# A decoder layer's feed-forward on one core: up for all tokens, then down, each with seven products in place of eight

## What is computed

```python
def _L0_ffn_ref(x, w1, s1, w2, s2, w3, s3):
    W1 = dequant_q40(w1, s1, hidden, dim)      # hidden = 2752, dim = 1024
    W3 = dequant_q40(w3, s3, hidden, dim)      # 4-bit words times a scale for 64 values
    W2 = dequant_q40(w2, s2, dim, hidden)
    a = jnp.einsum('bsd,hd->bsh', x, W1)
    b = jnp.einsum('bsd,hd->bsh', x, W3)
    h = jax.nn.silu(a) * b
    return jnp.einsum('bsh,dh->bsd', h, W2)
...
x = x + _L0_ffn_ref(_layernorm(x, axis=-1), ...)
```

## Time and profile before

| | |
|---|---|
| median of 3 runs | 3304.04 us (3301.68 to 3304.31) |
| profiled execution, its time from first to last instruction (span) | 3302.6 us |
| profiled span against the median | 1.4 us less |
| PE busy | 3132.5 us, 95% |
| DVE, ACT, POOL busy | 54%, 32%, 15% |
| mean granted clock of PE | 0.976 of full speed |
| stage of the feed-forward | 1806.6 to 3302.6 us |

### The profile page before, as it was taken

One profiled execution on the slowest core, in us unless ns is written; L12 is line 12 of the kernel. 1 busy time (PEld: TensorE's weight loads), 2 busy tenths in 40 slices (PEclk: granted clock), 3 DMA queues, 4 the chain that ended last, 5 costly groups with the idle time before them and its releaser, 6 DMA issues. The chain is left out here.

```text
span 3302.6 us, 41842 instructions
## 1 busy us (share of the span) xinstructions
PE 3132.5 (95%) x15136; PEld 2396.3 (73%) x15136; DVE 1772.9 (54%) x2927; ACT 1045.8 (32%) x2356; POOL 506.7 (15%) x525
## 2 busy tenths in 40 slices
PE   7999998799999999999996799999999899999999
PEld 6888886566666666666663688888887788888887
DVE  5311112466666666666663655555555655555555
ACT  2100000566666566666651211111111211111111
POOL 2100000233333333333332100000000100000000
PEclk9999999899999999999997899999999999999999
DMA  4222223111111111111110422222122521222222
GB/s 143 93 71 74 73 73 109 48 39 38 38 51 48 40 38 39 50 38 51 38 33 25 134 82 54 72 65 80 54 81 73 153 66 54 81 81 54 61 75 78
DMA packets 83350, 218.73 MB, mean 66 GB/s; under 512 B 11984, under 2 KB 18256, under 8 KB 81232
## 3 DMA queue, kind: packets, MB, share of 16 engines
q1 hardware_dynamic: 83280, 217.78, 21.7%
HBM read 175.79 MB, written 41.94 MB: 66 GB/s over the span
## 5 line engine op out<-in xcount | busy, mean ns | idle before, releaser
L1042 ACT ACTIVATE w_hi<-words 128x1024 fp32r<-128x1024 f32 x134 | 142.5, 1064 | 697.5 <-DVE words L1087 697.5
L312 PE MATMUL ff_ps<-h_xT_hi,w_hi 128*128 128x512 f32 x1376 | 344.0, 392 | 13.2 <-DVE h_xT_lo L96 13.2
L1127 DVE TENSOR_TENSOR acc<-ff_po,acc 128x512 f32<-128x512 f32 x352 | 243.0, 692 | 210.0 <-PE ff_po L1214 209.3
L312 PE MATMUL ff_ps<-h_xT_lo,w_hi 128*128 128x512 f32 x1376 | 341.8, 391 | 0.0
L312 PE MATMUL ff_ps<-h_xT_hi,w_lo 128*128 128x512 f32 x1376 | 339.8, 389 | 0.0
L312 PEld LDWEIGHTS ff_ps<-h_xT_hi,w_hi 128*128 128x128 f32 x1376 | 259.8, 189 | 68.4 <-issue 8.8
L312 PEld LDWEIGHTS ff_ps<-h_xT_lo,w_hi 128*128 128x128 f32 x1376 | 260.0, 189 | 54.4
L312 PEld LDWEIGHTS ff_ps<-h_xT_hi,w_lo 128*128 128x128 f32 x1376 | 258.3, 188 | 53.6
L282 DVE TENSOR_SCALAR qkv_out<-qkv_acc 128x512 f32<-128x512 f32 x96 | 66.4, 692 | 396.5 <-PE qkv_acc L312 396.5
L1115 DVE TENSOR_TENSOR gate<-gate,ff_ps 128x512 f32<-128x512 f32 (+1 forms) x88 | 60.3, 686 | 345.4 <-PE ff_ps L312 344.6
L656 ACT ACTIVATE scores<-scores,neg_max 128x128 f32<-128x128 f32 x512 | 199.1, 390 | 122.6 <-DVE neg_max L487 122.6
(11 more groups left out here) (156 smaller groups left out, 5196.5 us busy)
## 6 DMA issues: line engine op xcount, KB each, us to landing
words<-in_w SPq DMA_DIRECT2D x90, 512.0 KB, 3.5
qkv<-qkv_out SPq DMA_DIRECT2D x96, 256.0 KB, 2.0
words<-in_w SPq DMA_DIRECT2D x176, 128.0 KB, 4.0
sc<-in_s SPq DMA_DIRECT2D x88, 256.0 KB, 4.3
qk_in<-qkv SPq DMA_DIRECT2D x16, 1024.0 KB, 5.0
w_stage<-in_w_attn SPq DMA_DIRECT2D x56, 256.0 KB, 2.9
qkv_rows<-in_x SPq DMA_DIRECT2D x16, 512.0 KB, 3.8
ctx_in<-in_context SPq DMA_DIRECT2D x16, 512.0 KB, 3.8
```

What stands on the lines that cost most here:

```text
L312: last = nc.tensor.matmul(out, left, right, start=n == 0, stop=n == len(pairs) - 1)
L1042: nc.scalar.activation(dst, src, ACT.Copy).then_inc(s["split_hi"], 1)
L1127: nc.vector.tensor_tensor(cols, po[:, o % 4, :], cols, ALU.add).then_inc(s["added"], 1)
```

## The change

One level of Strassen's algorithm, in Winograd's form with chained sums, is applied to both products. The stage becomes two passes.

**Up.** A hidden tile's weights W1 and W3 form the columns of a 2 x 2 block matrix whose rows are the two halves of the features; the tokens' block matrix has the two halves of the features and the two halves of the 1024 tokens. Seven products of 4 feature slices x 3 passes give the four PSUM sums. The operands of the products are the blocks and sums of them: three sums of the weights before and one behind `w_low` 4, on POOL (`w_sums`, `w_last_sum`), and four sums of the tokens, once in each half (`x_sums`). ACT and DVE split seven operands of 128 x 512 for each tile. Products 0, 2, 4, 6 are accumulated in one PSUM bank (`X`), and what it holds is taken out in between: ACT copies it (`r1`, `r2`; also bank `B`, `p5`), DVE adds. h is not used at once: of two tiles' h POOL makes four sums (`h_sums`), and seven 128 x 512 pieces go to DRAM (`hc`). The second half's rows are normalised and transposed during the first half's tiles 2 to 17 (`prepared`), kept in DRAM (`xc`), and loaded in the place of the first half's between the halves (`refill`).

**Down.** 84 steps (`STAGES`): 6 groups of 4 hidden tiles (the last has 2), 2 halves, 7 products. A step takes one h piece from DRAM, splits it (ACT, then the low part on POOL, `g_low`), makes 4 banks of 6 matmuls (3 in the last group), and DVE adds each to `acc`, which now holds all 2048 tokens. W2's operands are shifted, scaled, summed and split once for each group.

Two buffers (`rows`) take the token rows in turn, and a row is loaded again only when its buffer's transposition is done (`load_x` waits for `x_turned`). The four `x_sums` of a quarter are chained like the `h_sums`. The core of the diff, in the order SP, POOL, ACT, DVE, PE:

```diff
-            feed_forward_phase(nc, sb, pb, sem, holds, ph, w13, s13, w2, s2, shifts, x2, out, ident, half_neg,
-                               ln_stats, ln_moments)
+            feed_forward_phase(nc, pb, sem, ph, w13, s13, w2, s2, shifts, x2, hc, xc, out, ident, half_neg, ln_stats,
+                               ln_moments, shift)
...
+    X_ORDER = [A11, A12, A22, S3, S1, S2, S4]
...
+    REFILL = [S2, S3, S4, A11, S1, A22, A12]
...
+    STAGES = [(c, hf, st) for c in range(6) for hf in range(2) for st in range(7)]
...
+                else:
+                    sp.wait_ge(s["x_lo"], 28 + r - 1)
+                sp.dma_start(refill[r % 2], xc[:, :, X_RAW[REFILL[r]], :].rearrange("i p f -> p i f")).then_inc(
+                    s[f"refill_in{r % 2}"], 16)
...
+            def load_acc(q):
+                sp.wait_ge(s["mm"], n_mm(1, LAST) + q + 1)
+                sp.dma_start(acc[:, 4 * q:4 * q + 4, :], x2[4 * q:4 * q + 4, :, :].rearrange(
+                    "t p d -> p t d")).then_inc(s[f"acc_in{q}"], 16)
...
+            for n in range(2):
+                load_x(n)
...
+            load_w(0, 0)
+            for n in range(2, 4):
+                load_x(n)
+            load_w(1, 1)
...
+                        for k in range(2):
+                            load_raw(k)
+                        load_acc(0)
+                        load_raw(2)
+                        load_acc(1)
+                        load_raw(3)
+                        load_acc(2)
+                        load_acc(3)
...
+            for k, (c, hf, st) in enumerate(STAGES):
+                if k + 5 < len(STAGES):
+                    load_raw(k + 5)
+                if c < 5 and hf == 0:
+                    tiles = [4 * c + 4 + j for j in range(2 * width(c + 1))]
+                    if st == 0:
+                        sp.wait_ge(s["v_lo"], c * 7 + 7)
+                        for j, tile in enumerate(tiles):
+                            load_v(tile, j)
+                        load_v_scale(tiles[0], 0)
+                    if 3 <= st < len(tiles) + 2:
+                        load_v_scale(tiles[st - 2], st - 2)
...
+            def h_sums(hf, m):
...
+                nc.gpsimd.tensor_tensor(hb[:, 5, :], hb[:, 0, :], hb[:, 3, :], ALU.subtract).then_inc(s["h_sums"], 1)
+                pool.wait_ge(s["h_sums"], n * 4 + 1)
+                nc.gpsimd.tensor_tensor(hb[:, 3, :], hb[:, 3, :], hb[:, 2, :], ALU.add).then_inc(s["h_sums"], 1)
...
+            def w_sums(hf, u):
...
+                pool.wait_ge(s["scaled"], n_scaled(hf, u) + 2)
+                if u:
+                    pool.wait_ge(s["w_lo"], n_w(hf, u - 1) + 3)
+                elif hf:
+                    pool.wait_ge(s["w_lo"], n_w(0, LAST) + 2)
+                nc.gpsimd.tensor_tensor(w_t[0][:, :, :], b12, b11, ALU.subtract).then_inc(s["w_sums"], 1)
+                pool.wait_ge(s["w_sums"], n + 1)
+                nc.gpsimd.tensor_tensor(w_t[1][:, :, :], b22, w_t[0][:, :, :], ALU.subtract).then_inc(s["w_sums"], 1)
+                nc.gpsimd.tensor_tensor(b12, b22, b12, ALU.subtract).then_inc(s["w_sums"], 1)
...
+            for n in range(2):
+                normalise(n)
+            for i in range(4):
+                if i < 3:
+                    normalise(2 * i + 2)
+                    normalise(2 * i + 3)
+                else:
+                    w_sums(0, 0)
+                x_sums(i, xr if i % 2 == 0 else hb)
+            w_last_sum(0, 0)
+            for hf in range(2):
+                for u in range(NT):
+                    m, e = u // 2, u % 2
+                    after = (hf, u + 1) if u < LAST else (1, 0) if hf == 0 else None
+                    if e == 0 and (m or hf):
+                        h_sums(hf if m else 0, m - 1 if m else PAIRS - 1)
+                    if after:
+                        w_sums(*after)
+                    if prepared(hf, u) is not None and e:
+                        normalise(prepared(hf, u))
+                    if after:
+                        w_last_sum(*after)
+                    if prepared(hf, u) is not None and e and m % 2 == 0:
+                        x_sums(3 + m // 2, xr)
+            for k in range(3):
+                g_low(k)
+            v_sums(0)
+            h_sums(1, PAIRS - 1)
+            v_last_sum(0)
...
+            def full(hf, u, after, ahead):
+                m, f = n_mm(hf, u), n_full(hf, u)
+                act.wait_ge(s["mm"], m + 1)
+                act.wait_ge(s["h0"], f)
+                nc.scalar.activation(a0[:, :], X[u % 2], ACT.Copy).then_inc(s["r1"], 1)
+                w_high(*after, 0)
+                act.wait_ge(s["mm"], m + 2)
+                act.wait_ge(s["h1"], f)
+                nc.scalar.activation(b1[:, :], B, ACT.Copy).then_inc(s["p5"], 1)
+                w_high(*after, 1)
+                act.wait_ge(s["mm"], m + 3)
+                nc.scalar.activation(b0[:, :], X[u % 2], ACT.Copy).then_inc(s["r2"], 1)
+                w_high(*after, 2)
+                if u < LAST - 1:
+                    w_high(*after, 3)
+                act.wait_ge(s["c11"], f + 1)
+                nc.scalar.activation(a0[:, :], a0[:, :], ACT.Silu).then_inc(s["gated0"], 1)
+                if u < LAST - 1:
+                    w_high(*after, 4)
+                    w_high(*after, 5)
+                if ahead is not None:
+                    copy_x(ahead)
+                if hf == 0 and u == LAST - 1:
+                    refill_high(0)
+                act.wait_ge(s["mm"], m + 7)
+                nc.scalar.activation(a1[:, :], X[u % 2], ACT.Silu).then_inc(s["gated1"], 1)
+                if u < LAST - 1:
+                    w_high(*after, 6)
...
+            for k in range(3):
+                g_high(k)
+            v_high(0, 0)
+            last_gate(1, 1)
+            v_high(0, 1)
+            last_gate(1, 0)
+            g_high(3)
+            for st in (2, 3, 4, 5, 6):
+                v_high(0, st)
...
+            def full(hf, u, after, ahead):
+                m, f, e = n_mm(hf, u), n_full(hf, u), u % 2
+                n = hf * PAIRS + u // 2
+                plain = u < LAST - 1
+                unpack(*after)
+                for p in range(3):
+                    w_low(*after, p)
+                dve.wait_ge(s["mm"], m + 4)
+                dve.wait_ge(s["r1"], f + 1)
+                nc.vector.tensor_tensor(a0[:, :], C, a0[:, :], ALU.add).then_inc(s["c11"], 1)
+                if plain:
+                    w_low(*after, 3)
+                elif hf == 0:
+                    unpack(1, 0)
+                dve.wait_ge(s["mm"], m + 5)
+                dve.wait_ge(s["p5"], f + 1)
+                nc.vector.tensor_tensor(b1[:, :], X[e], b1[:, :], ALU.add).then_inc(s["c22"], 1)
+                if plain:
+                    w_low(*after, 4)
+                dve.wait_ge(s["mm"], m + 6)
+                dve.wait_ge(s["r2"], f + 1)
+                nc.vector.tensor_tensor(b0[:, :], B, b0[:, :], ALU.add).then_inc(s["c12"], 1)
+                if plain:
+                    w_low(*after, 5)
+                if n:
+                    dve.wait_ge(s["hb_a_out"], n * 16)
+                    dve.wait_ge(s["h_sums"], n * 4)
+                dve.wait_ge(s["gated0"], f + 1)
+                dve.wait_ge(s["c12"], f + 1)
+                nc.vector.tensor_tensor(hb[:, e, :], a0[:, :], b0[:, :], ALU.mult).then_inc(s["h0"], 1)
+                if ahead is not None:
+                    statistics(ahead)
+                if hf == 0 and u == LAST - 1:
+                    refill_low(0)
+                if n:
+                    dve.wait_ge(s["hb_b_out"], n * 16)
+                dve.wait_ge(s["gated1"], f + 1)
+                dve.wait_ge(s["c22"], f + 1)
+                nc.vector.tensor_tensor(hb[:, 2 if e else 3, :], a1[:, :], b1[:, :], ALU.mult).then_inc(s["h1"], 1)
+                if plain:
+                    w_low(*after, 6)
...
+            for i in range(4):
+                if i < 3:
+                    statistics(2 * i + 2)
+                x_low(i, 0, 3)
+                if i < 3:
+                    statistics(2 * i + 3)
+                x_low(i, 3, 7)
+                if i == 3:
+                    w_low(0, 0, 0)
+                    w_low(0, 0, 1)
...
+            for k, (c, hf, st) in enumerate(STAGES):
+                sl, par = TO[st]
+                if c == 0 and st in (0, 3):
+                    dve.wait_ge(s[f"acc_in{hf * 2 + (st == 3)}"], 16)
+                for tp in range(4):
+                    t = hf * 8 + sl * 4 + tp
+                    dve.wait_ge(s["mm2"], k * 4 + tp + 1)
+                    if k:
+                        dve.wait_ge(s["added"], (k - 1) * 4 + tp + 1)
+                    nc.vector.tensor_tensor(cols, banks[:, (0 if k % 2 else 4) + tp, :], cols, ALU.add).then_inc(
+                        s["added"], 1)
+                if k < 2:
+                    for slot in ((2, 3), (4, 5, 6))[k]:
+                        v_low(0, slot)
```

(36 more changed lines are left out.)

## The result

The changed kernel takes 3342.7 us in the median of 4 runs (3337.16 to 3344.12), and the kernel before, run beside it, 3303.1 us (3301.68 to 3304.31): a ratio of 1.0118, 95% interval 1.0103 to 1.0132. It is 40 us slower where 80 less were forecast, outside the range. The profiled span is 3335.4 us, against 3222.0 in the forecast's sum. The profiled execution of the changed kernel is the shortest of its four runs, 5.5 us under their median; the profiled executions of the experiments lie within 3.2 us of theirs.

The account below looks back on a forecast made before the run. PE's matmul count was taken as the bound. 1239.4 us of matmuls plus 72 + 8 + 55 + 6 + 11 + 16 + 8 gave 1415.4 in place of 1496.0 us, so 3223 us in all; range 3155 to 3285.

Parts of the forecast that it names:

- the 6 of the token sums: Up, four pairs of tiles: the second half's x sums stand ahead of the h sums, 1.5 us each, 6 us.
- the 11 of the change: Between up's halves: seven 1 MB operands reloaded through two buffers make PE wait, 11 us with clock loss.
- the joint's 16: From up to down: late first product 10 us, step 3 late 3 us, late load of step 6 3 us.
- What is removed: Both products: 768 fewer matmuls at 0.2265 us each, 174 us; 5472 left, 1239.4 us.
- p4's wait in even tiles: Up: PE's product p4 waits for r2, behind POOL's sums, 2.6 us in 21 even tiles, 55 us.
- POOL's price of 1.17 us: A POOL sum of two full 128x512 operands, taken as half a 128x1024 one; bounds 1.04 and 2.35 us.
- The other eight tiles are transposed inside products, about 1.0 us each at full clock: Second half's token tiles, transposed on PE during up: 8 us in all.
- PE bound: Down after its start: a step has 5.44 us of PE against about 4.1 of DVE with unpacking, 3.0 of POOL.
- The clock: Low PE clock priced at two places: 2.7 us at the first products, 2.6 at the change of halves.
- Rival (b): Up: the clock falls at each of the 21 p4 waits, price 55 us, time 3278 us; chance 0.10.
- Change of halves, start, joint and end: Stage's edges: change of halves 11 us, start +35 us, up to down 16 us, end 8 us.
- Rival (c): Up: POOL's sums take 2.35 us, p4 waits 8.5 and the clock falls, 3395 us, slower than before; chance 0.10.

Follow-up runs that it names:

- experiment 5: POOL's four h sums cut to 8 of 512 columns, orders and waits unchanged, against the changed kernel: 3265.9 us, ratio 0.9888 to the kernel before.
- experiment 3: PE transposes the second half's rows behind product p5 instead of p3, against the changed kernel: 3304.9 us, ratio 1.0006 to the kernel before.
- experiment 4: Four scale buffers in down instead of one, each loaded with its words, against the changed kernel: 3312.2 us, ratio 1.0028 to the kernel before.
- experiments 1 to 3: Each against the changed kernel: r2 copied before ACT's high part, 3305.3 us; weight sums before h sums on POOL, 3303.4; transposes behind p5, 3304.9.

## Why the prediction was wrong

What failed is not the wait that the forecast was about but three terms beside it: the clock (5.3 us in the sum, 63.1 measured), the operand of the transposes in the first half of up (nothing, 20.6), and the waits in down (6, 30.8).

By pieces of the stage, in us, for the profiled execution. The forecast's pieces are the prediction's own terms: up's 3624 products and p4's 55 are split evenly between the halves, the first has the 6 of the token sums, the 8 of the transposes and the 2.7 of the clock, the second the 11 of the change, and of the joint's 16 down has 6:

| piece | forecast | measured |
|---|---|---|
| to the first product (1881.4) | 69.5 | 74.8 |
| up, first half | 454.6 | 500.0 |
| up, second half, with the change | 448.9 | 464.6 |
| up to down | 10 | 11.8 |
| down | 424.6 | 469.0 |
| end | 8 | 8.6 |
| sum | 1415.6 | 1528.8 |

- **What is removed:** right, in count and in time of one. The stage at full clock without waits would need 1239.4 us plus the transposes, as forecast.
- **p4's wait in even tiles:** right in mechanism, and nearly in size. 55 + 6 were forecast and 56.7 measured, nearly all in 20 waits: 2.02 us against 2.1 to 2.8 in a plain tile, and with the token sums 3.2 more, not 1.5. `r2` ended 12.8 us into the tile (2458.17; the tile began at 2458.31 - 2.02 - 4 x 2.72 = 2445.4), forecast 13.0 to 13.7. POOL's price of 1.17 us was low: alone the sum takes 1.29, beside DVE mostly up to 2.16, at most 2.29. The Trainium skill, SBUF — State Buffer, section "SBUF: two separate sides", has the two engines lock each other out for a whole instruction; the shift of 2.32 us against 1.34, and its return to 1.34 in experiment 5, agree, and for the shift too, where I had been in doubt.
- **"The other eight tiles are transposed inside products, about 1.0 us each at full clock":** failed. That costed PE's work and not its operand. Eight times the normalisation, queued on POOL behind the weight sums, came 2.57 to 2.64 us late: 20.6 us, and in experiment 3 these waits and 13.5 us of slow clock went together.
- **"PE bound" in down:** failed. DVE was weighed by its busy time, 4.1 against 5.44 us a step, though the code has one scale buffer and its load behind loads that wait for POOL. 30.8 us of idle time (469.00 - 438.19) against 6 forecast; 25.5 of it is DVE's additions, which experiment 4 removed.
- **The clock:** failed, and it is the largest of the three. The sum had 5.3 us for it, at the two places with long idle times. Measured: PE's busy time in the three pieces less the work at full clock (447.2 + 425.1 + 438.2 = 1310.5, less 1239.4 and 8) is 63.1 us. The earlier trace rows had one wait of 2.62 with hardly any loss, and I took all such waits as harmless from that one case. Rival (b), with its 0.10, is partly right: it had a loss behind all 21 waits of p4. Half clock followed 11 of the 20, and it also followed 5 of the transposes' 8 waits and all 9 at the change and in down of 3.12 us and more. From 2446 to 2545 us, with three waits of 2.02 and one stretch behind them, the clock is 0.98; in the first half, with transposition and p4 waiting in each pair, it was 0.94.
- **Change of halves, start, joint and end:** 14.5 us of idle time at the change against 8.4 without the clock, 5.3 late at the start, 1.8 and 0.6 at the others; small, of one sign.

By size: clock 57.8 beyond the forecast, transposes' waits 20.6, down's waits 24.8, start 5.3, change 6.1, joint and end 2.4, p4 -4.3: 112.7 of the 113.4 us between 3222.0 and 3335.4. A loss needed 81 us over the forecast, by its own working; 113 came, from places of 5 to 58 us each that I had at nothing or too low. The waits that I left out also brought clock loss of their own, as experiment 3 shows. Rival (c), which came out on the right side, had another mechanism: sums of 2.35 us in a row. The 128x512 sums took 2.35 nowhere: 1.29 without DVE beside them, where (c) needed over 1.5; beside DVE up to 2.29, in series with it, as the forecast already had them.

## What to carry to other kernels

When a change takes the slack out of PE's stream, ask of each instruction on PE, the small ones too, when its operand is ready by the queue of the engine that makes it, and of each engine's queue what it waits for ahead of the work that frees PE's banks: busy sums per step showed neither. Many waits of 2 to 3 us cost more than their idle time, through the clock: experiments 1 to 3 removed 18.0, 15.3 and 17.8 us of idle time and 11.5, 15.9 and 13.5 of slow clock with it. Here the gain of 7 in place of 8 products was real and lay behind three orders in queues and a buffer; none of the mends needed less arithmetic.

## What the runs showed of the hardware

- In the changed kernel half clock followed all 14 waits of PE of 3.12 us and more, 5 of the 8 of 2.57 to 2.64, 6 of the 14 of 2.02 to 2.26, and none of the 5 of 1.02 to 1.90. So a wait of 2.02 us can be enough.
- How near the next wait is does not decide it: the four waits from 1935 to 2002 us, some 22 us apart, had none behind them, and of eight of 2.58 to 2.64 us, 43 us apart, in experiment 5 seven had. What decides for waits of 2 to 3 us stays open.
- A POOL sum of 128x8 takes 1.17 us beside DVE's shift and scaling and 0.20 at the least in the same run, while a 128x512 one alone takes 1.29. Beside DVE, a short POOL operation is priced by what DVE is doing.
